# State-space stage of a four-stage model kernel: the ring of products with B has four slots in place of eight

## The chip, the cores and the metric

The kernel runs on one core of a Trainium2 chip. The metric is the device time of one execution in microseconds (us). The engines are TensorE (PE in the profile, with PEld for its weight loads), VectorE (DVE), ScalarE (ACT), GpSimd (POOL) and SyncE (SP), which here issues the DMAs.

## What is computed

Two layers on x of shape (8, 512, 256), in float32. The change lies in the first: a Mamba block and an FFN with 4-bit weights and activations, both added to x.

```python
xz = jnp.einsum('bld,ed->ble', x, W_in);  x_in, z = xz[..., :512], xz[..., 512:]
xc = silu(causal_conv4(x_in) + conv_b)                       # u
x_dbl = u @ W_xproj.T                                         # 16 + 16 (B) + 16 (C) columns
delta = softplus(x_dbl[..., :16] @ W_dt.T + b_dt)
A = -exp(A_log)
def step(h, inp):                                             # over the 512 positions
    d_t, u_t, B_t, C_t = inp
    dA = jnp.exp(d_t[:, :, None] * A[None])
    h = dA * h + (d_t * u_t)[:, :, None] * B_t[:, None, :]
    return h, jnp.einsum('bdn,bn->bd', h, C_t)
y = (ys + D_param * u) * silu(z);  return y @ W_out.T

# the FFN: fp4_quant_dequant rounds blocks of 16 values onto a 4-bit grid under the block's maximum
gate, up = fp4_linear(x, w_gate), fp4_linear(x, w_up)
return fp4_linear(silu(gate) * up, w_down)
```

The second layer (block-sparse attention plus a two-layer local-attention network) is two later stages of the kernel, which the change doesn't touch.

## The kernel before

`build` runs four stages one after the other: preparing the FFN's weights, `mamba_and_fp4_ffn` (the state-space stage), `block_sparse_attention` and `local_attention_layers`. Within a stage every engine has an instruction stream written out by hand, with explicit waits on semaphores.

The state-space stage goes over 8 batches. A batch is 32 steps, numbered 0 to 31 here: 4 groups of 128 channels (`c`) by 8 groups of two states (`g`). The recurrence runs along the free dimension, so one step treats 128 channels by 2 states by 512 positions, a tile of 128x1024. Per step s:

- SP spreads two rows of B and two of C over 128 partitions by DMA, into `bcB` and `bcC`, each with four slots (`ROWS`). A slot of B is loaded again once the product that read it is done (L422), a slot of C once the weighing that read it is done (L427). The two kinds alternate in SP's queue.
- POOL multiplies B by delta*u, L560: `hb[s % RING] = bcB * du`. This is called the product of step s. Before it POOL waits for B, and for the sum that last read the slot: L557, `summed` of step s - RING.
- ACT writes exp(delta * A) into one of two PSUM slots `dA`, two ACTIVATEs, L823; it waits until the weighing of step s - 2 is done.
- DVE scans, L662: h = dA * h + hb, result in `dA` (PSUM); then it weighs, L673: `hb[s % RING] = dA * bcC`.
- PE adds the two state rows of `hb[s % RING]` into `ps_y` through an identity matrix: two matmul calls, four MATMUL records, L1049. This is called the sum of step s; it increments `summed`. After the eight sums of a channel group DVE gates them by silu(z), L624 (in steps 8, 16 and 24, and in step 0 of the next batch).

So a ring slot goes product, scan, weighing, sum, and then to the product RING steps on.

Everything else is laid between these by tables of step numbers: the input projection, convolution and softplus of the next batch, and the FFN of the current one. What touches the prediction:

- DVE quantises the FFN's hidden rows in `fp4_part`. A block of rows takes three consecutive steps, each part between a scan and the weighing: part 0 (L640 gating, then L124 to L128: block maxima, scale, inverse), part 1 (L131 to L133), part 2 (L135, L136). The four blocks start at steps 3, 22, 25 and 28 (`HIDDEN`). The FFN's input goes through the same three parts at steps 12, 15 and 17 (`XQ`), for the next batch. L125, L126, L128, L131, L135 and L136 are TENSOR_TENSOR with both inputs in SBUF; L132 and L133 are TENSOR_SCALAR on SBUF. The scan and the weighing read `dA` from PSUM.
- POOL also does, in its own order of steps: delta's last addition, L517; delta*u, L552, ahead of products 0, 8, 16 and 24; the scaling of quantised blocks, L107, after products 8, 20, 27 and 30 and after product 31, each time waiting for DVE's part 2; and the layer norm (L506 to L512) after product 3.
- `prepare` on ACT, PE and DVE works for the next batch, and is absent in the last one.

Of the kernel before, what the change touches and what calls it, by code (L numbers as in the profile page):

```python
# [221 lines left out]
def mamba_and_fp4_ffn(nc, io, W, x1_dram, bc_dram, NB):  # L222
# [10 lines left out]
    NG = 2  # L233
    GROUPS = NS // NG
    SCANS = GROUPS * IC
    RING, ROWS = 8, 4

# [2095 lines left out]
def build(nc, io, out, NB):  # L2335
    x1_dram = nc.dram_tensor("x1_scratch", [NB, 512, 256], F32).ap()
    bc_dram = nc.dram_tensor("bc_scratch", [NB, 33, 512], F32).ap()
    base_dram = nc.dram_tensor("base_scratch", [NB, 512, 256], F32).ap()
    stream = nc.dram_tensor("stream_scratch", [2, NB, 512, 256], F32).ap()
    with ExitStack() as ctx:  # L2340
        W = {"ident": ctx.enter_context(nc.sbuf_tensor("ident", [P, P], F32))}
        with ExitStack() as first:
            for name, shape in (("gateT", [P, 2, 704]), ("upT", [P, 2, 704]), ("downT", [P, 6, 256])):
                W[name] = first.enter_context(nc.sbuf_tensor(name, shape, F32))
            prepare_fp4_weights(nc, io, W)
            mamba_and_fp4_ffn(nc, io, W, x1_dram, bc_dram, NB)
        block_sparse_attention(nc, io, W, x1_dram, stream[0], base_dram, NB)
        local_attention_layers(nc, io, W, stream, base_dram, out, NB)
# [70 lines left out]
```

How the kernel before makes its waits and increments, by code:

```python
    def link(self, ins):  # L63
        self.eng.wait_ge(self.s, self.at(self.done(ins)))
# [50 lines left out]
def fp4_part(dve, st, rows, blk, work, cst, p, n, part):  # L115
    g = n // 16
    amax, scale, inv = blk[0:p, 0, 0:g], blk[0:p, 1, 0:g], blk[0:p, 2, 0:g]
    w = work[0:p, 0:n]
    blocks = rows.rearrange("p (g e) -> p g e", e=16)
    if part == 0:
        sixth, least, under = (bc(cst[0:p, i:i + 1], [p, g]) for i in range(3))
        st.link(dve.tensor_reduce(amax, blocks, AX.X, ALU.max, apply_absolute_value=True))
        st.link(dve.tensor_tensor(scale, amax, sixth, ALU.mult))
        st.link(dve.tensor_tensor(scale, scale, least, ALU.max))
        st.link(dve.reciprocal(inv, scale))
        return st.done(dve.tensor_tensor(inv, inv, under, ALU.mult))
    if part == 1:
        dve.wait_ge(st.s, st.at(st.k))
        st.link(dve.tensor_tensor(blocks, blocks, bc(inv.unsqueeze(2), [p, g, 16]), ALU.mult))
        st.link(dve.tensor_scalar(w.bitcast(U32), rows.bitcast(U32), EXPONENT, None, ALU.bitwise_and))
        return st.done(dve.tensor_scalar(w, w, 1.0, 1.5 * 2.0 ** 22, ALU.max, ALU.mult))
    dve.wait_ge(st.s, st.at(st.k))
    st.link(dve.tensor_tensor(rows, rows, w, ALU.add))
    return dve.tensor_tensor(rows, rows, w, ALU.subtract)
# [32 lines left out]
        @block.gpsimd  # L169
        def _(pool):
            pool.memset(W["ident"][:, :], 0.0).then_inc(ident0, 1)
            pool.wait_ge(ident0, 1)
            pool.affine_select(out=W["ident"][:, :], in_=W["ident"][:, :], compare_op=ALU.not_equal, fill=1.0,
```

## Time and profile before

| | us |
|---|---|
| median of 3 runs | 3743.01 |
| lowest and highest | 3740.74, 3743.61 |
| the profiled execution, its own time | 3745.46 |
| its span, first to last instruction | 3743.4 |
| busy: PE | 3272.0 (87%) |
| busy: DVE | 2609.0 (70%) |
| busy: ACT | 1655.2 (44%) |
| busy: POOL | 1582.9 (42%) |

The busy shares are means over stages with different limits. The 256 scans, one a step, start between 136.7 us and 1492.8 us of the span; that is the stage in which the change lies. The second stage's instructions on DVE follow after 1499.7 us. A time of an engine's operation, such as 923.00, is counted from the span's start. All work between 828.51 us (the fifth batch's first scan) and 1002.46 us (the sixth's) is called the fifth batch below.

### The profile page before, as it was taken

To read this page: it belongs to the slowest core of one execution; us is meant where nothing else is said; L and a number is where in the kernel's file an instruction comes from. 1 tells how busy PE (TensorE), PEld (TensorE's weight loads), DVE (VectorE), ACT (ScalarE), POOL (GpSimd) and SP (SyncE) were. 2 spreads that over 40 slices of the span, in tenths; PEclk is the share of its full clock that TensorE was granted. 3 is DMA by queue.
4 is the path that set the end of the run, shared out by engine and by line. 5 is a ranking of instruction groups with operands and counts; after the bars stand their busy time and mean duration, and the time that the engine had idled before them with its cause. 6 is when DMAs were issued, how large, how long until landed. Compare 5 with 4: busy or idle time off the path is not lost. (4 is left out here: it accounts for less than half of the span.)

```text
span 3743.4 us, 50627 instructions
## 1 busy us (share of the span) xinstructions
PE 3272.0 (87%) x16204; PEld 1892.7 (51%) x16204; DVE 2609.0 (70%) x3818; ACT 1655.2 (44%) x4071; POOL 1582.9 (42%) x977
## 2 busy tenths in 40 slices
PE   2788888889898987799999869999999689999998
PEld 1234344444444443466666536666666356666665
DVE  5599999999999999476777545555555255555553
ACT  1464545455454644365566423333333133333332
POOL 1556464556555554000000045444454165555552
PEclk9799999999998999899999979999999799999999
DMA  1466565656565665100110010000000200000000
GB/s 48 166 211 212 192 215 188 211 192 226 177 226 176 223 209 179 54 23 22 34 34 17 25 65 17 17 17 17 17 17 12 70 18 23 22 22 22 22 17 18
DMA packets 146680, 343.51 MB, mean 92 GB/s; under 512 B 14898, under 2 KB 78470, under 8 KB 146582
## 3 DMA queue, kind: packets, MB, share of 16 engines
q1 hardware_dynamic: 138134, 334.02, 26.6%
q10 hardware_dynamic: 8448, 8.39, 0.7%
q8 instruction: 37, 0.61, 0.1%
q14 instruction: 61, 0.50, 0.0%
HBM read 320.87 MB, written 21.50 MB: 91 GB/s over the span
## 5 line engine op out<-in xcount | busy, mean ns | idle before, releaser
L1049 PE MATMUL ps_y<-hb,ident 128*128 128x512 f32 x1024 | 548.9, 663 | 182.1 <-DVE hb L673 180.9
L662 DVE TENSOR_TENSOR_SCAN ps_dA<-ps_dA,hb 128x1024 f32<-128x1024 f32 x256 | 585.6, 2288 | 76.7 <-ACT ps_dA L823 76.7
L560 POOL TENSOR_TENSOR hb<-bcB,du 128x1024 f32<-128x1024 f32 x256 | 597.3, 2358 | 37.7 <-DMA bcB<-bc_scratch 31.2
L1049 PEld LDWEIGHTS ps_y<-hb,ident 128*128 128x128 f32 x1024 | 195.9, 204 | 437.1 <-DVE hb L673 254.2
L1834 POOL TENSOR_TENSOR c_pr<-c_pr,c_inv 128x512 f32<-128x512 f32 (+1 forms) x256 | 233.8, 935 | 384.3 <-DVE c_inv L1959 382.4
L1403 ACT ACTIVATE b_pr<-b_ps_s,b_negmax 128x256 f32<-128x256 f32 (+1 forms) x512 | 263.8, 527 | 166.2 <-DVE b_negmax L1317 164.8
L2317 PE MATMUL c_ps_s<-c_hT,c_w 128*128 128x512 f32 x704 | 322.1, 604 | 17.2 <-DVE c_hid L2025 15.4
L823 ACT ACTIVATE ps_dA<-delta,a_neg 128x511 f32<-128x511 f32 x512 | 329.8, 675 | 0.7
L2077 ACT ACTIVATE c_pr<-c_ps_s,c_negmax 128x256 f32<-128x256 f32 (+1 forms) x512 | 222.0, 449 | 222.0 <-DVE c_negmax L1941 149.5
L673 DVE TENSOR_TENSOR hb<-ps_dA,bcC 128x1024 f32<-128x1024 f32 x256 | 312.0, 1219 | 4.3
L1811 POOL TENSOR_TENSOR c_q_cos<-c_q_cos,c_q_sin 128x1024 f32<-128x1024 f32 x64 | 150.8, 2357 | 311.4 <-DVE c_q_sin L1920 311.4
L821 ACT ACTIVATE ps_dA<-nought 128x2 f32<-128x2 f32 x256 | 44.4, 173 | 534.4 <-DVE hb L673 533.3
L1317 DVE TENSOR_REDUCE b_negmax<-b_ps_s 128x2 f32<-128x512 f32 (+1 forms) x320 | 204.5, 683 | 73.4 <-PE b_ps_s L1474 72.4
L2165 PE MATMUL c_ps_s<-c_w_qkv,c_xT 128*128 128x512 f32 x512 | 241.4, 616 | 1.4 <-ACT c_xT L2050 1.4
L1261 POOL TENSOR_TENSOR b_xb<-b_xb,b_o_bias 128x1024 f32<-128x1024 f32 x8 | 18.8, 2349 | 498.7 <-DMA b_xb<-x_scratch 498.7
L2317 PEld LDWEIGHTS c_ps_s<-c_hT,c_w 128*128 128x128 f32 x704 | 129.8, 193 | 178.2 <-issue 148.6
L1488 PE MATMUL b_ps_t<-ident,b_pr 128*128 128x128 f32 x1280 | 190.1, 286 | 24.7 <-DVE b_pt L1339 12.8
L2025 DVE SCALAR_TENSOR_TENSOR c_hid<-c_ps_s,c_b_cols,c_gl 128x512 f32<-128x512 f32 x96 | 70.5, 746 | 197.4 <-ACT c_gl L2130 178.1
L1817 POOL TENSOR_TENSOR c_rn<-c_ssc,c_mhalf 128x16 f32<-128x16 f32 x64 | 186.4, 2913 | 31.8 <-DVE c_ssc L1930 31.3
L1488 PEld LDWEIGHTS b_ps_t<-ident,b_pr 128*128 128x128 f32 x1280 | 137.1, 142 | 113.9 <-DVE b_pt L1339 55.7
L2056 ACT ACTIVATE c_sq<-c_ps_s 128x512 f32<-128x512 f32 x128 | 69.5, 595 | 256.5 <-PE c_ps_s L2165 256.5
L1474 PE MATMUL b_ps_s<-b_kf,b_qm 32*128 32x256 f32 (+1 forms) x1024 | 177.3, 460 | 0.9 <-ACT b_kf L1376 0.9
(244 smaller groups left out, 6364.9 us busy)
## 6 DMA issues: line engine op xcount, KB each, us to landing
bcB<-bc_scratch SPq DMA_DIRECT2D x256, 512.0 KB, 4.8
bcC<-bc_scratch SPq DMA_DIRECT2D x256, 512.0 KB, 3.9
c_x<-stream_scratch SPq DMA_DIRECT2D x16, 512.0 KB, 5.0
c_xr<-stream_scratch SPq DMA_DIRECT2D x16, 512.0 KB, 4.5
xn<-in_x_dram SPq DMA_DIRECT2D x8, 512.0 KB, 5.1
xr<-in_x_dram SPq DMA_DIRECT2D x8, 512.0 KB, 5.9
x_scratch<-xr SPq DMA_DIRECT2D x8, 512.0 KB, 4.9
b_x<-x_scratch SPq DMA_DIRECT2D x8, 512.0 KB, 4.1
```

The costliest lines, as they stand in the source:

```text
L560: pool.tensor_tensor(hb[:, s % RING, :, :], bcB[:, s % ROWS, :, :], bc(du[:, c % 2, :].unsqueeze(1), [P, NG, T]), ALU.mult)\
L662: dve.tensor_tensor_scan(flat(h_all), flat(h_all), flat(tile), 0.0, ALU.mult, ALU.add)\
L673: dve.tensor_tensor(tile, h_all, bcC[:, s % ROWS, :, :], ALU.mult).then_inc(weighed.s, 1)
L823: last = act.activation(dA[:, s % 2, n, 1:], delta[:, c, 1:], ACT.Exp, scale=a_neg[:, c, g * NG + n:g * NG + n + 1])
L1049: last = pe.matmul(ps_y[:, :], W["ident"][:, :], hb[:, r % RING, i, :], start=False, stop=(g == GROUPS - 1 and i == terms - 1))
L1317: dve.tensor_reduce(negmax[:, u, 0:heads], ps_s[:, u % 4, :].rearrange("p (h n) -> p h n", h=heads), AX.X, ALU.max, negate=True).then_inc( ...
L1403: last = act.activation(pr[:, u % 8, cols], ps_s[:, u % 4, cols], ACT.Exp, bias=negmax[:, u, i:i + 1], accum_out=den[:, qt, h:h + 1])
L1488: last = pe.transpose(ps_t[:, u % 2, k * P:(k + 1) * P], pr[:, u % 8, k * P:(k + 1) * P], W["ident"][:, :])
L1834: pool.tensor_tensor(rows, rows, bc(inv[:, u, :].unsqueeze(2), [P, 2, w]), ALU.mult)\
L2077: last = act.activation(pr[:, u % 6, i * w:(i + 1) * w], ps_s[:, u % 4, i * w:(i + 1) * w], ACT.Exp, scale=-1.0 if s < AHEAD else 1.0, bia ...
L2165: last = pe.matmul(ps_s[:, pair(t) + a, :], xT[:, k, t * P:(t + 1) * P], w_qkv[:, k, a * INNER:(a + 1) * INNER], start=(k == 0), stop=(k = ...
L2317: last = pe.matmul(ps_s[:, pair(j) + a, :], w_1[:, k, at:at + P], hT[:, k, :], start=(k == 0), stop=(k == DC - 1))
```

## The change

```diff
@@ -233,7 +233,7 @@
     NG = 2
     GROUPS = NS // NG
     SCANS = GROUPS * IC
-    RING, ROWS = 8, 4
+    RING, ROWS = 4, 4
```

`hb` is allocated as `[P, RING, NG, T]`, so it shrinks from 32 KiB to 16 KiB a partition. Slots are numbered `s % RING` in the product, the scan, the weighing and the sum alike. The product of step s now waits for the sum of step s - 4 in place of s - 8, across batches too (the first four products of a batch wait for sums 28 to 31 of the one before). Every engine issues the same operations on the same shapes in the same order as before; what differs is which sum the wait of L557 (or L559, across batches) names.

## Rows read from the trace of the kernel before

**Rows 1.** Windows: busy us (instructions) of PE, PEld, DVE, ACT, POOL; PEclk; DMA share, GB/s

```profile
137.00:1499.00 1362.00, 1159.23 (x3127) 570.16 (x3126) 1272.06 (x1029) 715.49 (x1284) 765.43 (x403) 0.93 0.60 203
```

**Rows 2.** Waits of VectorE, 137 to 1499: us in total, times, longest

```profile
DVE ps_dA L662 <- ACT ps_dA L823: 76.7, 17, 45.6
DVE y L624 <- PE ps_y L1049: 23.5, 15, 3.2
```

**Rows 3.** Waits of GpSimd, 137 to 1499

```profile
POOL h L107 <- DVE h L136: 260.4, 25, 13.6
POOL delta L517 <- ACT xin L698: 164.1, 15, 17.0
...
POOL hb L560 <- PE ps_y L1049: 0.7, 2, 0.5
```

**Rows 4.** Timeline of GpSimd, fifth batch: start, us, line; x3 are products 21-23, 24-26, 28-30

```profile
921.11 1.93 POOL L107 TENSOR_TENSOR xn<-xn,blk_x 128x1024 f32<-128x1024 f32 x1 [12.90 <-DVE xn L136]
923.00 6.98 POOL L560 TENSOR_TENSOR hb<-bcB,du 128x1024 f32<-128x1024 f32 x3
...
931.56 6.98 POOL L560 TENSOR_TENSOR hb<-bcB,du 128x1024 f32<-128x1024 f32 x3 [0.23 <-DMA bcB<-bc_scratch]
...
960.41 6.95 POOL L560 TENSOR_TENSOR hb<-bcB,du 128x1024 f32<-128x1024 f32 x3
```

**Rows 5.** Timeline of VectorE, fifth batch, steps 25 (L125 to L128) and 4 (L131 to L133)

```profile
960.42 2.40 DVE L125 TENSOR_TENSOR blk_h<-blk_h,cst 128x44 f32<-128x44 f32 x1
962.85 2.27 DVE L126 TENSOR_TENSOR blk_h<-blk_h,cst 128x44 f32<-128x44 f32 x1
...
965.62 1.80 DVE L128 TENSOR_TENSOR blk_h<-blk_h,cst 128x44 f32<-128x44 f32 x1
...
851.99 2.06 DVE L131 TENSOR_TENSOR h<-h,blk_h 128x704 f32<-128x704 f32 x1
854.08 1.47 DVE L132 TENSOR_SCALAR work<-h 128x704 uint32<-128x704 uint32 x1
855.59 2.54 DVE L133 TENSOR_SCALAR work<-work 128x704 f32<-128x704 f32 x1
```

**Rows 6.** Timeline of VectorE, fifth batch: scan 21, then steps 22 (L125) and 23

```profile
932.55 2.29 DVE L662 TENSOR_TENSOR_SCAN ps_dA<-ps_dA,hb 128x1024 f32<-128x1024 f32 x1
...
943.17 0.20 DVE L125 TENSOR_TENSOR blk_h<-blk_h,cst 128x44 f32<-128x44 f32 x1
...
947.56 0.87 DVE L131 TENSOR_TENSOR h<-h,blk_h 128x704 f32<-128x704 f32 x1
948.47 0.53 DVE L132 TENSOR_SCALAR work<-h 128x704 uint32<-128x704 uint32 x1
...
949.47 1.22 DVE L673 TENSOR_TENSOR hb<-ps_dA,bcC 128x1024 f32<-128x1024 f32 x1
```

**Rows 7.** Timeline of TensorE, fifth batch: sums 16 and 17 (x8), 21, 23, 24

```profile
921.46 3.60 PE L1049 MATMUL ps_y<-hb,ident 128*128 128x512 f32 x8
...
941.12 1.88 PE L1049 MATMUL ps_y<-hb,ident 128*128 128x512 f32 x4
...
950.75 1.98 PE L1049 MATMUL ps_y<-hb,ident 128*128 128x512 f32 x4 [1.94 <-DVE hb L673]
...
957.04 1.88 PE L1049 MATMUL ps_y<-hb,ident 128*128 128x512 f32 x4
```

**Rows 8.** TensorE after step 4 of the fifth batch: its timeline, and the window with the clock

```profile
859.32 3.78 PE L1049 MATMUL ps_y<-hb,ident 128*128 128x512 f32 x4 [6.76 <-DVE hb L673]
...
855.00:866.00 11.00, 6.68 (x13) 4.03 (x14) 10.93 (x8) 3.62 (x9) 5.26 (x4) 0.53 0.38 126
```

**Rows 9.** Step 3 of the fourth batch: timelines of VectorE and of GpSimd

```profile
669.26 8.40 DVE L125 TENSOR_TENSOR blk_h<-blk_h,cst 128x44 f32<-128x44 f32 x1
...
670.64 6.95 POOL L560 TENSOR_TENSOR hb<-bcB,du 128x1024 f32<-128x1024 f32 x3
```

**Rows 10.** Step 25 of the last batch: timeline of VectorE

```profile
1461.35 2.27 DVE L126 TENSOR_TENSOR blk_h<-blk_h,cst 128x44 f32<-128x44 f32 x1
```

## The prediction

> **What bounds the kernel now.** The change touches one stage, so I read the windows first: in its 1362 us VectorE is busy 1272.06, GpSimd 765.43, TensorE 1159.23 [rows 1]. VectorE sets the pace. Its waits come next: 76.7 us for ScalarE's exponentials (45.6 of it once, at the start) and 23.5 for sums before the gating [rows 2]; none for a product of GpSimd. GpSimd's own waits say why: it sits 260.4 us waiting for VectorE's quantising and 164.1 for ScalarE, and only 0.7 for a sum, the wait that the change tightens [rows 3]. It runs far ahead: products 24 to 26 are made from 931.56 on, in one go [rows 4], while VectorE is at scan 21 (932.55) [rows 6].
>
> By those views four slots cost nothing. The next one, VectorE's timeline with GpSimd's beside it, says otherwise. L125 takes 0.20 us at step 22 [rows 6], but 2.40, L126 2.27 and L128 1.80 at step 25 [rows 5], exactly while GpSimd makes products 28 to 30, from 960.41 for 6.95 us [rows 4]. L131 takes 0.87 alone and 2.06 under a product, L132 0.53 and 1.47; L133, which is as long as L132, 2.54 [rows 5, 6]. So a quantising operation of VectorE ends no earlier than the GpSimd instruction in progress. Scan (2.29) and weighing (1.22), which read PSUM, keep their length under products. "Busy" hides this: held time counts as VectorE's work.
>
> The Trainium skill, page "SBUF — State Buffer", section "Who interferes with whom", calls it an exclusive lock on a port pair that the two engines share; whoever starts first keeps it for the whole instruction, and a VectorE operation with two SBUF inputs, or in a two-port mode, contends for it. These rows agree.
>
> **The change part by part.** No instruction is added or removed, and each product lasts as before, 6.98 / 3 = 2.33 us [rows 4]. What moves is when products run. All steps below are of the fifth batch.
>
> *When a product now starts.* Not before the sum of four steps back. An unhindered sum takes 1.98 us and starts 0.06 after its weighing ends (950.75 [rows 7], against 949.47 + 1.22 [rows 6]). So its product starts some 2.1 us after a weighing. VectorE's next scan starts at once and takes 2.29, some 0.2 of it overlapped, so the quantising operation behind it is issued 2.1 us after the same weighing. This coincidence is the heart of the matter: the new wait lines products up with the moments when VectorE wants the port. Which of the two is first matters little: if the product, L131 is held; if L131, the product waits for it and L132 is held for all of the product, 2.54 - 0.53 = 2.0, as L133 was at step 4 [rows 5, 6].
>
> *Step 22.* Product 20 starts with sum 16's end, 921.46 + 1.88 = 923.3 [rows 7], and ends at 925.7; L107 takes 1.93 [rows 4]; product 21 ends near 930.0; products 22, 23 and 24 follow sums 18, 19 and 20; product 25 starts with sum 21's end, 941.12 + 1.88 = 943.0 [rows 7]. L125 is issued at 943.17 [rows 6] and held to 945.3: **+2.15**.
> *Step 23.* Weighing 22 ends later by that, so TensorE has cleared its queue, sum 22 is unhindered, and product 26 meets L131: **+2.1**.
> *Step 24.* The gating comes first and covers most, only L136 is left to be held: 0 to 2.0, **+0.8**.
> *Step 25.* Products 28 to 30 no longer run in one go. Held today: 2.40 + 2.27 + 1.80 - 3 x 0.20 = 5.87 [rows 5, 6]. Left is product 28, from sum 24's end at 957.04 + 1.88 = 958.9 [rows 7] to 961.25, against L125 at 960.42 [rows 5]: 0.8. **-5.1**.
> *Step 26.* The sum takes between 1.98 and 3.78 [rows 7, 8], so the product starts 2.1 to 3.9 us after the weighing, and L131 to L133 fill 2.1 to 4.1: one hold at any of these, **+2.0**.
> *Step 28.* Again a part 0. Between step 25's 0.8 and step 22's 2.15: **+1.5**.
> *Step 4.* Held today (2.06 - 0.87) + (1.47 - 0.53) + (2.54 - 0.53) = 4.1 [rows 5, 6], by products 7, L552 and product 8. Product 7 (2.1) and L552 (0.9) still collide, product 8 waits for sum 4: **-1.1**.
> *Steps 3, 5, 12, 15, 17.* At step 3 the layer norm delays products 4 and 5 more than any sum does. At the others one collision replaces another, or the sum ends when the part is over: **0**.
> A batch: 2.15 + 2.1 + 0.8 - 5.1 + 2.0 + 1.5 - 1.1 = +2.35, with 0.7 more if step 28 is hit in full. I take **+2.6**.
>
> *The clock and the gatings.* Behind a stall of VectorE TensorE stands idle: after step 4 it waits 6.76 us, and the next stretch runs at a granted clock of 0.53, near the lower level of 1.2 GHz, four matmuls taking 3.78 in place of 1.98 [rows 7, 8]. Late TensorE work is then waited for by gatings and by ScalarE [rows 2]. Steps 22/23, 26 and 28 get such stalls, step 25 loses one. Bounds: 0, and 3 x (3.78 - 1.98) = 5.4. I take **+3**, just above the middle, since a gating stands right behind two of the stalls.
>
> *Two long waits.* In the third and fourth batch L125 at step 3 is held 8.40 us, through three products back to back from 670.64 on [rows 9]; in the others it isn't. Product 7, the last of the three, must now wait for sum 3, which comes after L125's own step, so each such wait is at least 2.33 shorter. TensorE's catching up gives part of these waits back already: **-4** for both, between 0 and -9. By the lock page's "whole instruction" L125 would have got in at the end of the GpSimd instruction under way, and the term would be 0; the row shows that it waited through several.
>
> *The last batch.* It has no preparation and few holds: four, 5.6 us over the free times, the longest L126's 2.27 [rows 10]. Its products will follow sums from 4 on, so its parts at steps 4, 5 and 22 to 28 are hit as above, and there is little to lose: **+10**, 5 to 12.
>
> *What costs nothing.* Scans still find their products: the tightest is 21, done near 930.0 against scan 21 at 932.55 [rows 6], 2.5 us in hand. A row of B waits for the product four back, which is earlier than the sum four back. A row of C for step s + 4 is queued on SP behind product s + 2, which is done before scan s + 2, over two steps ahead of its use. Delta's additions behind products 15 and 17 slip with them, but ScalarE wants their results at steps 16 and 24, and starts those after weighings 14 and 22, later than sum 11 and sum 13.
>
> Sum: 7 x (2.6 + 3) - 4 + 10 = **+45 us**, to 3745.46 + 45 = 3790.5 for the profiled execution. That one lies 2.45 above the median of 3743.01, so the median goes to **3788**.
>
> **The rivals.** 0.2% either way, 7.5 us, is about what a measurement of this kernel can tell from no change.
> - *The bursts were the harm* (faster). Products could fall into scans or behind the parts, if sums end less than 0 or over 4 us behind the time at which VectorE is ready for its part at steps 22, 23, 26 and 28. Then a batch gains 5.1 + 1.1 and pays nothing: 7 x -6.2 - 4 = -47, 3696. For it: TensorE's queue varies by several us. Against it: sum 21 ends 0.17 us ahead of L125, and an unhindered sum 2.04 behind its weighing [rows 6, 7]. Chance 0.06.
> - *The collisions only move* (no change). A third of the new ones (2.8 us a batch) miss and the clock costs nothing: 7 x (2.6 - 2.8) + 7 - 4 = +2, 3745. Nor would the ring matter if it didn't bind; but product 21 alone starts 2 us ahead of sum 17's end (923.00 against 921.46 + 3.60) [rows 4, 7]. Chance 0.09.
> - *Products become late for scans.* If sums 16 and 17 slip by over 2.5 us, scan 21 waits, in each batch. With 2 us more 7 x 2 = 14 on top, 3802; with the upper clock bound, 7 x 2.4 = 17, 3819. Chance 0.15.
> - *Forecast*: 0.70.
>
> **How the numbers follow.** The forecast's own bounds: clock at 0, last batch 5, long waits -9 give 7 x 2.6 + 5 - 9 = +14, 3757; clock at 5.4, last batch 12, long waits 0 give 7 x 8 + 12 = +68, 3811. The range is 3757 to 3814: it leaves out the faster case, the unchanged one and the tip of the third. Slower by over 0.2%: the forecast and the third, 0.85, and a hundredth of the second. Within 0.07, faster 0.07.
>
> **What would show it.** After the change GpSimd's largest wait is for sums, and no three products run in one go at steps 21 to 26. L125 at step 22 and L131 or L132 at step 23 take over 2 us; L126 and L128 at step 25 return to 0.20. VectorE still doesn't wait for products, and waits more for sums. A batch in the middle takes 179 to 180 us from first scan to first scan, now 1002.46 - 828.51 = 173.95. The later stages keep their time. It is wrong if the quantising lines' total doesn't grow, or if scans wait for products.

## The result and the profile after

The changed kernel takes 3805.36 us, median of 4 runs, against 3742.80 for the kernel before: ratio 1.0159, 95% interval 1.0137 to 1.0182. That is +62.6 us; the forecast was +45, 3788, in a range of 3757 to 3814, so slower by more than forecast and inside the range. Three of the four runs lie within 0.5 us of each other; the fourth took 3792.08, and nothing here explains it. The profiled execution's span grew from 3743.4 to 3803.5 us, by 60.1.

All of it is in the state-space stage. Its windows row, with the columns of [rows 1]:

```profile
138.00:1559.00 1421.00, 1187.51 (x3126) 584.13 (x3125) 1296.70 (x1028) 713.24 (x1284) 796.11 (x403) 0.92 0.57 194
```

The stage is 59 us longer (1421 against 1362), with VectorE 24.6 busier and the same operations. Behind the last weighing the kernel takes as long as before, 2247.2 against 2247.0 us. The last batch alone, from its first scan to the last weighing, grew from 146.8 to 157.1 us. Waits of VectorE and then of GpSimd in the stage, as in [rows 2, 3]:

```profile
DVE ps_dA L662 <- ACT ps_dA L823: 94.2, 16, 47.2
DVE y L624 <- PE ps_y L1049: 41.1, 21, 3.1
...
POOL hb L560 <- PE ps_y L1049: 430.2, 146, 6.6
POOL h L107 <- DVE h L136: 94.4, 11, 11.4
POOL delta L517 <- ACT xin L698: 48.3, 7, 6.9
```

GpSimd now waits 430.2 us for sums, before 0.7. VectorE still never waits for a product; it waits 17.5 us more for exponentials and 17.6 more for sums.

The fifth batch now starts at 856.77. VectorE's timeline there at steps 22 to 25, and then step 26, which answers to [rows 5, 6]:

```profile
970.77 2.32 DVE L125 TENSOR_TENSOR blk_h<-blk_h,cst 128x44 f32<-128x44 f32 x1
973.12 0.20 DVE L126 TENSOR_TENSOR blk_h<-blk_h,cst 128x44 f32<-128x44 f32 x1
...
977.27 0.88 DVE L131 TENSOR_TENSOR h<-h,blk_h 128x704 f32<-128x704 f32 x1
978.18 2.54 DVE L132 TENSOR_SCALAR work<-h 128x704 uint32<-128x704 uint32 x1
...
986.45 0.69 DVE L624 TENSOR_TENSOR y<-ps_y,z 128x512 f32<-128x512 f32 x1 [1.82 <-PE ps_y L1049]
...
987.97 1.84 DVE L136 TENSOR_TENSOR h<-h,work 128x704 f32<-128x704 f32 x1
...
994.89 0.85 DVE L125 TENSOR_TENSOR blk_h<-blk_h,cst 128x44 f32<-128x44 f32 x1
995.77 0.20 DVE L126 TENSOR_TENSOR blk_h<-blk_h,cst 128x44 f32<-128x44 f32 x1
...
1001.40 2.55 DVE L133 TENSOR_SCALAR work<-work 128x704 f32<-128x704 f32 x1
```

And GpSimd's, products 25 and 26, with TensorE's sum 23 and the window around it (columns of [rows 1]):

```profile
970.68 2.34 POOL L560 TENSOR_TENSOR hb<-bcB,du 128x1024 f32<-128x1024 f32 x1 [2.09 <-PE ps_y L1049]
977.28 3.06 POOL L560 TENSOR_TENSOR hb<-bcB,du 128x1024 f32<-128x1024 f32 x1 [4.25 <-PE ps_y L1049]
...
982.47 3.78 PE L1049 MATMUL ps_y<-hb,ident 128*128 128x512 f32 x4 [5.27 <-DVE hb L673]
...
982.40:986.50 4.10, 4.03 (x5) 1.49 (x6) 2.28 (x3) 4.01 (x5) 0.00 (x0) 0.50 0.73 239
```

Product 25 starts 0.09 us ahead of L125, which is held to the product's end. Product 26 starts 0.01 behind L131: now the product waits for L131 (3.06 us in place of 2.35) and L132, which follows at 978.18 and takes 2.54 us, is held in turn. TensorE, idle for 5.27 us because of that hold, is back at the lower level of its clock (granted 0.50): sum 23 takes 3.78 us, where it took 1.98 before [rows 7], and the gating L624, which waited for nothing there before, stands 1.82 for it.

### The profile page after: what moved, and what is told of

Same layout as the page of the kernel before. It is cut to its first block and busy times, and to the rows that moved or that the text cites. A ratio compares the mean times of both kernels' runs of the same rounds, so it can differ in the third digit from the quotient of the medians.

```text
span 3803.5 us, 50631 instructions
## 1 busy us (share of the span) xinstructions
PE 3303.7 (87%) x16204; PEld 1908.2 (50%) x16204; DVE 2633.8 (69%) x3818; ACT 1652.8 (43%) x4071; POOL 1613.0 (42%) x977
## 5 line engine op out<-in xcount | busy, mean ns | idle before, releaser
L560 POOL TENSOR_TENSOR hb<-bcB,du 128x1024 f32<-128x1024 f32 x256 | 619.7, 2428 | 435.5 <-PE ps_y L1049 430.2
L1049 PE MATMUL ps_y<-hb,ident 128*128 128x512 f32 x1024 | 563.8, 678 | 212.5 <-DVE hb L673 211.2
L1488 PE MATMUL b_ps_t<-ident,b_pr 128*128 128x128 f32 x1280 | 190.2, 286 | 24.7 <-DVE b_pt L1339 12.7
```

The lines of the kernel that those rows point to most:

```text
L560: pool.tensor_tensor(hb[:, s % RING, :, :], bcB[:, s % ROWS, :, :], bc(du[:, c % 2, :].unsqueeze(1), [P, NG, T]), ALU.mult)\
L1049: last = pe.matmul(ps_y[:, :], W["ident"][:, :], hb[:, r % RING, i, :], start=False, stop=(g == GROUPS - 1 and i == terms - 1))
L1488: last = pe.transpose(ps_t[:, u % 2, k * P:(k + 1) * P], pr[:, u % 8, k * P:(k + 1) * P], W["ident"][:, :])
```

## The experiments

Two theories. *Meetings*: the cost is when products run. The wait for sum s - 4 puts them beside VectorE's quantising, which a GpSimd instruction in progress holds up; everything else, idle TensorE at a low clock included, follows from the holds. (*Held* means that an operation takes longer than its shortest duration, while a GpSimd instruction runs.) *Ring*: four slots cost on their own account, by the memory's place, by products or sums that come late, or evenly by each wait of GpSimd. Each experiment is given by its median, beside that of the kernel before in the same runs. One scan 0 to the next, from the second batch on, is 172.1 to 175.9 us before and 180.8 to 181.2 after.

### The wait alone, the slots alone

```diff
-                        if s >= RING:
-                            pool.wait_ge(summed.s, summed.at(b, s - RING + 1))
+                        if s >= 4:
+                            pool.wait_ge(summed.s, summed.at(b, s - 4 + 1))
```

with the line across batches changed alike and `RING` at 8. For the slots alone `RING` is 4 and the memory is kept:

```diff
-        hb = sb("hb", [P, RING, NG, T])
+        hb = sb("hb", [P, 2 * RING, NG, T])
```

> Eight slots as before, but the product of step s waits for the sum of step s - 4. If the cost is when products run, this equals the changed kernel: +62 us against the kernel before (+55 to +66), fifth batch 180.9 us. If it is the smaller buffer (other addresses, nearer reuse), this stays within 5 us of the kernel before.

> Four slots are used, but memory for eight is allocated, so that all tensors behind it keep the addresses of the kernel before. If the cost is the waiting, +62 us as in the changed kernel; if it is where the tensors lie in SBUF, some of it is gone.

Measured, before at 3743.24: the wait alone 3809.34, ratio 1.0179 (1.0159 to 1.0199); four slots in the old memory 3807.06, ratio 1.0175 (1.0155 to 1.0194). Both intervals overlap the change's. So neither the nearer reuse of a slot nor the addresses of the tensors behind the ring matter, the wait for the sum four back does. The Ring theory loses its first part.

### Quantising that can't be held

In `fp4_part` eight operations (the expectation below says nine) give way to reductions of nearly the same length. These two kernels leave the rounding of the activations out. In part 0 and part 1:

```diff
-        return st.done(dve.tensor_tensor(inv, inv, under, ALU.mult))
+        return st.done(dve.tensor_reduce(inv, amax.unsqueeze(2), AX.X, ALU.max))
...
-        st.link(dve.tensor_tensor(blocks, blocks, bc(inv.unsqueeze(2), [p, g, 16]), ALU.mult))
-        st.link(dve.tensor_scalar(w.bitcast(U32), rows.bitcast(U32), EXPONENT, None, ALU.bitwise_and))
-        return st.done(dve.tensor_scalar(w, w, 1.0, 1.5 * 2.0 ** 22, ALU.max, ALU.mult))
+        q = g // 2
+        half = blocks[:, 0:q + 1, :]
+        st.link(dve.tensor_reduce(inv, blocks, AX.X, ALU.max))
+        st.link(dve.tensor_reduce(inv[:, 0:q + 1], half, AX.X, ALU.max))
+        return st.done(dve.tensor_reduce(inv[:, 0:q + 1], half, AX.X, ALU.max))
```

> Eight slots; the nine operations of the activations' 4-bit quantising that GpSimd can hold up are replaced by TENSOR_REDUCEs of about the same lengths (0.2, 0.5 and 0.9 us), which the traces show at one length under a product and alone (so rows are not quantised, block maxima are computed in place). By the theory of holds all held time goes (about 137 us of VectorE's time in the profile of before) and the kernel takes about 3608 (3590 to 3630). If the holds are covered by other waits, it gains far less.

> The same replacement of the quantising, with four slots. By the theory of holds the ring's size costs nothing once no operation can be held: within 5 us of the run with eight slots and this replacement. If four slots also cost by late products, by sums waited for, or by TensorE's clock on their own account, it stays 20 to 60 us above it.

Measured, before at 3743.24: with eight slots 3620.75, ratio 0.9679 (0.9663 to 0.9696); with four 3619.97, ratio 0.9676 (0.9660 to 0.9692). VectorE's and GpSimd's rows of the kernel with four slots (lines by group: count, busy us, mean ns, idle; then a wait):

```profile
L133 DVE TENSOR_REDUCE blk_h<-h 128x44 f32<-128x704 f32 x32 | 27.5, 860 | 0.0
L134 DVE TENSOR_REDUCE blk_h<-h 128x23 f32<-128x368 f32 x32 | 17.2, 536 | 1.1
...
POOL hb L562 <- PE ps_y L1051: 305.6, 144, 5.4
```

GpSimd still waits 305.6 us for sums, and the kernel is no slower than with eight slots. VectorE still sets the pace there, busy 1146.6 of the 1237.0 us from the first scan to the last weighing, so a cost of the ring to VectorE would show. Take the possibility of a hold away, and the whole difference of 62.6 us goes. This is the experiment on which the account rests. It also shows that the kernel before pays some 122 us for holds and what follows from them: VectorE's busy time in that stretch falls by 125.7 us (from 1272.3), of which 124 are its held time before, so the reductions are hardly shorter than what they replace. The expectation's 137 us of held time were too many.

### Which products

The wait is four back only `if s < 20`, or only `if 25 <= s < 28`, else eight. The second:

```diff
+                        back = 4 if 25 <= s < 28 else RING
-                        if s >= RING:
-                            pool.wait_ge(summed.s, summed.at(b, s - RING + 1))
+                        if s >= back:
+                            pool.wait_ge(summed.s, summed.at(b, s - back + 1))
```

> Eight slots; only the products of steps 0 to 19 wait for the sum four back, the others for the one eight back. If what decides is which quantising part a product meets, these products cost little: the losses were put at steps 22 to 28, so within 10 us of the kernel before (sum of my terms 0). If the tight ring costs evenly, some 20/32 of 62: +39.

> Eight slots; only products 25, 26 and 27 wait for the sum four back. My terms for steps 22, 23 and 24 (2.15 + 2.1 + 0.8) with what they delay, less nothing at step 25, in seven batches and the last: +30 to +50 us from 3 products of 32. If the cost is spread evenly: +6.

Measured, before at 3740.75: the first twenty products 3749.00, ratio 1.0023 (1.0014 to 1.0033), +8; the three products 3785.61, ratio 1.0127 (1.0110 to 1.0144), +45. Three products of 32 carry some 70% of the loss, twenty others an eighth. An evenly spread cost is ruled out. In the three-product kernel VectorE's timeline shows steps 22 to 24 as in the changed one:

```profile
961.65 2.32 DVE L125 TENSOR_TENSOR blk_h<-blk_h,cst 128x44 f32<-128x44 f32 x1
...
969.07 2.54 DVE L132 TENSOR_SCALAR work<-h 128x704 uint32<-128x704 uint32 x1
...
977.33 0.69 DVE L625 TENSOR_TENSOR y<-ps_y,z 128x512 f32<-128x512 f32 x1 [1.82 <-PE ps_y L1050]
...
978.86 1.84 DVE L136 TENSOR_TENSOR h<-h,work 128x704 f32<-128x704 f32 x1
```

### Other distances

The wait of the first experiment with 6 and with 3 in place of 4.

> Eight slots, the product waits for the sum of step s - 6. Products of steps 24 to 26 then come 10 us or more ahead of a sum they now miss only slightly, so steps 22 and 23 stay free and step 25 keeps its holds: within 10 us of the kernel before. If each slot less costs, half of 62: +31.

> Eight slots, the product waits for the sum of step s - 3. If only the meetings count, the total changes with the pattern and not in proportion: +65 to +90. If scans begin to wait for products (2.5 us in hand at step 21, a step is 3.5), VectorE's waits show hb L560 and it is +90 or more.

Measured, before at 3738.21: six back 3745.23, ratio 1.0019 (1.0010 to 1.0029), +7; three back 3808.26, ratio 1.0187 (1.0170 to 1.0204), +70. The cost jumps between six and four (five wasn't tried) and hardly rises from four to three, though GpSimd's wait for sums goes 51.6, 430.2, 595.9 us. At three back scans do begin to wait for products; VectorE's waits up to the last gating:

```profile
DVE ps_dA L662 <- ACT ps_dA L823: 90.3, 22, 46.4
DVE y L624 <- PE ps_y L1049: 31.0, 23, 3.1
DVE ps_dA L662 <- POOL hb L560: 16.0, 14, 2.6
```

16.0 us of it. I had put the kernel at "+90 or more" if that came, and it was +70; the gatings' waits are 10.1 us less than at four back. So the third rival's mechanism exists one slot further on, but not with four.

### Products timed to miss the quantising

If meetings are the cost, letting each product start later, at the right moment, must gain. The product of step s also waits until VectorE is through with its part (or its scan, in a step without one) of step s - 3, so that it runs beside a weighing and a scan:

```diff
+                        q, at = (s - 3) % SCANS, b if s >= 3 else b - 1
+                        if s >= 3 or prev:
+                            h_part = [(t, q - HIDDEN[t]) for t in range(TT) if HIDDEN[t] <= q < HIDDEN[t] + 3]
+                            if h_part:
+                                t, part = h_part[0]
+                                if part == 2:
+                                    pool.wait_ge(hg_ready.s, hg_ready.at(at, t + 1))
+                                else:
+                                    pool.wait_ge(h_steps.s, h_steps.at(at, t * FP4_PART_STEPS + (5, 8)[part]))
...
+                            else:
+                                pool.wait_ge(scanned.s, scanned.at(at, q + 1))
```

> Eight slots, and the product of step s also waits until VectorE has ended its quantising part (where there is none, its scan) of step s - 3, so that it runs beside a weighing and a scan, which aren't held. More waiting than in the kernel before, but by the theory of holds nearly all held time goes: 3640 us (3620 to 3665), about 100 below the kernel before. If waiting of GpSimd is what costs, it is slower than the changed kernel.

> The same timing of the products with the change's four slots, so both waits. By the theory of holds 3640 to 3670 us, up to 20 above the run with eight slots, since products whose sum is late still meet a part.

Measured, before at 3740.75: 3643.10, ratio 0.9742 (0.9725 to 0.9758), with eight slots; 3651.57, ratio 0.9765 (0.9748 to 0.9781), with four. The first is the fastest version here that computes the whole kernel, 98 us below the kernel before and 162 below the changed one, and with the change's four slots it still gains 89. Step 22 of its fifth batch, VectorE and then GpSimd:

```profile
882.49 0.20 DVE L125 TENSOR_TENSOR blk_h<-blk_h,cst 128x44 f32<-128x44 f32 x1
882.72 0.20 DVE L126 TENSOR_TENSOR blk_h<-blk_h,cst 128x44 f32<-128x44 f32 x1
...
883.42 0.20 DVE L128 TENSOR_TENSOR blk_h<-blk_h,cst 128x44 f32<-128x44 f32 x1
883.54 1.22 DVE L690 TENSOR_TENSOR hb<-ps_dA,bcC 128x1024 f32<-128x1024 f32 x1
...
883.71 2.36 POOL L577 TENSOR_TENSOR hb<-bcB,du 128x1024 f32<-128x1024 f32 x1 [5.81 <-DVE blk_h L128]
```

GpSimd waits 5.81 us for L128 and starts with the weighing. L132's 32 operations take 527 ns each, against 708 before and 1471 after the change. More waiting in sum, which the expectation named, there isn't: from the first scan to the last weighing GpSimd is idle for 493 us, before for 596. Its products begin later in their steps, and the steps are shorter.

## Why the prediction was right, and which terms were mis-sized

**The mechanism, the sign and the step numbers held.** By the forecast's steps, in the fifth batch (step 4 in the fourth), held time over the free length:

| step | forecast | measured |
|---|---|---|
| 4 (L132, L133) | 4.1 to 3.0 | 2.01 + 0.94 = 2.95 |
| 22 (L125) | +2.15 | 2.32 - 0.20 = 2.1 |
| 23 (L132) | +2.1 | 2.54 - 0.53 = 2.0 |
| 24 (L136) | +0.8 | 1.84 - 0.89 = 0.95 |
| 25 | 5.87 to 0.8 | 0.85 - 0.20 = 0.65 |
| 26 (L133) | +2.0 | 2.55 - 0.53 = 2.0 |
| 28 (L125) | +1.5, up to 2.15 | 2.22 - 0.20 = 2.0 |

An ordinary batch has 18.7 us of holds after the change, against 16.1 before (each quantising operation's length less its free length, summed over the batch): the +2.6 taken. Part of that is luck of cancelling: step 12 lost 1.3 of holds and step 15 gained 1.2, which I had both put at nothing. Over the stage holds rise from 123.8 to 148.5, by 24.7; the forecast's terms for them, 7 x 2.6 for the batches and +10 for the last, less what the long waits shrink by, give 19 to 28.

**The sum fell 15 us short on VectorE's idle time.** It rises by 35.9 us, from 132.9 to 168.8, waits of the first scan included. With the holds, 24.7 + 35.9 = 60.6, which is the span's 60.1 but for 0.5. Summed over the eight batches, the waits stand here:

| wait | before | after |
|---|---|---|
| scan 14, for exponentials | 4.9 | 13.8 |
| first scans, for exponentials | 71.3 | 79.9 |
| gatings at step 24, for sums | 1.6 | 14.3 |
| gatings at steps 8 and 16, for sums | 19.2 | 24.2 |
| steps 3, 22 and 28, for the FFN's matmuls | 20.0 | 21.0 |

**The largest error is the "0" for step 12.** The holds went there, about 1.5 us before and 0.15 after, but VectorE gained nothing, because scan 14 then stood 1.3 longer for ScalarE. Here is scan 14 in the fourth batch, before and then after, where scan 12 starts at 715.21 and at 734.68:

```profile
726.68 2.30 DVE L662 TENSOR_TENSOR_SCAN ps_dA<-ps_dA,hb 128x1024 f32<-128x1024 f32 x1 [0.66 <-ACT ps_dA L823]
...
746.15 2.30 DVE L662 TENSOR_TENSOR_SCAN ps_dA<-ps_dA,hb 128x1024 f32<-128x1024 f32 x1 [1.98 <-ACT ps_dA L823]
```

Both lie 11.47 us behind scan 12, a time that ScalarE's own work between them sets. So step 12's gain was no gain, nothing stood against step 15's 1.2, and 8.9 of the missing 15 us are this.

**"The clock and the gatings"**, +3 a batch, 21 in all, was nearly right. Leave out scan 14, the wait ahead of the very first scan (45.6 and 47.2) and the last batch (10.3 us longer in all, forecast +10), and some 23.5 of the 35.9 remain for it. At step 24 the clock's share can be read off: sum 23 starts as soon after its weighing as before and takes 1.8 us longer, and the gating waits 1.8 for it. The chain that I had left out runs into the next batch. Step 28's hold leaves TensorE idle for 4.39 us, the FFN's and the output's matmuls of steps 29 to 31 are late for ScalarE, and that makes the first scan's exponentials late. TensorE's and ScalarE's rows at the fifth batch's end, after the change:

```profile
1019.14 3.78 PE L1049 MATMUL ps_y<-hb,ident 128*128 128x512 f32 x4 [4.39 <-DVE hb L673]
...
1030.51 0.60 ACT L791 ACTIVATE xr<-ps_t 128x512 f32<-128x512 f32 x1 [4.76 <-PE ps_t L998]
```

And before:

```profile
985.12 3.58 PE L1049 MATMUL ps_y<-hb,ident 128*128 128x512 f32 x4 [2.45 <-DVE hb L673]
...
995.36 0.60 ACT L791 ACTIVATE xr<-ps_t 128x512 f32<-128x512 f32 x1 [3.62 <-PE ps_t L998]
```

TensorE lost its clock there before too (granted 0.58 from 985 to 989), but for a shorter stretch than after (0.50 from 1018 to 1024); ScalarE waits 1.1 us longer, and so does the first scan (3.63 to 4.76). How the rest divides between the clock and the order of work wasn't tried apart. That all of the change's cost follows from the holds is shown by the kernels whose quantising can't be held: there four slots cost nothing.

**The two long waits.** They didn't vanish. L125 at step 3 is again held long in two batches, now the fifth and the sixth, but through one product less:

```profile
873.20 6.08 DVE L125 TENSOR_TENSOR blk_h<-blk_h,cst 128x44 f32<-128x44 f32 x1
```

6.08 in place of 8.40, 2.32 shorter, as forecast ("at least 2.33 shorter"). These two batches take 180.8 and 180.9 us like their neighbours, where before they cost 2 us each; the -4 was right in sum. What decides whether L125 is held so long isn't shown. In the fifth batch steps 4 and 5 differ too: step 4 has no hold, and L136 at step 5 takes 2.92.

**"What costs nothing"** held for scans, rows of B and rows of C. For delta's additions it named the wrong reader: ScalarE also needs them at step 14, to overwrite `xin`, and waited there, which it never did before:

```profile
ACT xin L746 <- POOL delta L517: 45.3, 7, 6.5
```

Almost all of that wait is covered. The kernel with only the first twenty products tight has the same 45.3 us of it and loses 8 us in all, and the one with four slots and no holds has 38.4 and loses nothing.

**The rivals.** *The bursts were the harm* saw a gain that exists, and is larger than the 47 us that I gave it (98 with timed products, some 122 without holds), but it needs products timed to the parts, not to the sums. *The collisions only move* didn't come: all of the new holds came. Six slots' wait gives its time, 3745, but because that wait hardly binds (51.6 us). *Products become late* starts at three.

## What to carry to other kernels

"Busy" on VectorE can be waiting: compare one operation's shortest and longest durations by form, and lay the other engine's timeline beside the long ones. The depth of a ring sets when its producer runs, not only whether it is in time; a producer released by a consumer's event starts at the same phase of every step, and that phase may be the worst. Where two engines can hold each other up, release the producer on the event after which the other engine no longer minds, even if it could start earlier. And before a shorter operation is counted as a gain, look whether another engine's chain sets the next start anyway, as at scan 14.

## What the runs showed of the hardware that I had not expected

- A hold works both ways. A product that starts 0.01 us behind L131 takes 3.06 us in place of 2.35, and the next VectorE operation is held for as long as the product runs: 0.7 us of one engine and 2.0 of the other. Where the product is first by 0.09 us, it keeps its 2.34 and L125 loses 2.1.
- A held operation isn't always let in at the end of the GpSimd instruction under way. L125 at step 3, issued some 0.4 us before product 4's end, took 0.44 us in some batches and 8.40 (before) or 6.08 us (after) in others of the same execution: there it was held on through four (before) or three (after) more GpSimd instructions, which followed back to back. The Trainium skill's "SBUF — State Buffer", section "Summary: rules for kernel authors", has the second one to issue fully blocked "until the first finishes"; these rows show longer.
- TENSOR_REDUCE on SBUF keeps its length beside products (L124's median is 886 ns for 128x704, its longest 889, before and after the change alike), which made it a substitute for TENSOR_TENSOR (L131's is 874 before the change, its longest 2061).
